# Attention with a block-quantised feed-forward on one core: the work ahead of the first unit in another order, zeros multiplied in TensorE's waits, 22 chunks ahead instead of 24

## The chip, the cores and the metric

One Trainium2 chip, one core of it. The metric is the device time of the program in microseconds (us), the median of a few executions. The change is judged by that time against the kernel before.

## The reference, cut to what is computed

```python
def reference(inputs, Wq, bq, Wk, bk, Wv, bv, Wo, bo, w_gate, w_up, w_down):
    x = inputs                                    # (4, 1024, 128), float32
    xn = layernorm(x)
    # 16 heads of 8; rel[i, j] = pos[j] - pos[i] of one axis, so the bias is a row per head
    q, k, v = split_heads(xn @ Wq + bq), split_heads(xn @ Wk + bk), split_heads(xn @ Wv + bv)
    scores = einsum('bhqd,bhkd->bhqk', q, k) / sqrt(8) + alibi_slopes[:, None, None] * rel
    attn = einsum('bhqk,bhkd->bhqd', softmax(scores), v) @ Wo + bo
    # fp4_linear rounds both operands to a grid of 8 magnitudes, one scale for each 16 elements
    h = silu(fp4_linear(xn, w_gate)) * fp4_linear(xn, w_up)     # 352 wide
    return x + attn + fp4_linear(h, w_down)
```

## The kernel before

The core's four batches are worked off as 256 **units** (`NU`): batch, group of four heads (`quad`), half of the queries, and one of eight blocks of 128 keys. In unit U the stream on TensorE (`pe`) has two **chunks** (`half_chunk`, L1048: queries by all 1024 keys, for the row maxima alone), four **scores** (`score`, L1067) and the **value product** of unit U-1 (`value_product`, L1078). VectorE (`dve`) reduces each chunk to its row maxima (`reduce_chunk`, L934); a chunk has one of two PSUM slots `mx`, and TensorE may write a slot only when the reduction of what stood in it is done. ScalarE (`act`) takes the exponentials (L728). GpSimd (`pool`) does the quantising of the feed-forward and splits the maxima in two bf16 parts (`max_parts`, L630 and L631), which TensorE turns (`turn`, L1056) and SyncE's DMA queue (`sp`) brings into the operands `q_op` by way of DRAM.

The chunks run ahead of the scores: `LEAD` = 24 chunks are done before unit 0 starts.

All other work is a **job**, put into the middle or the end of a unit by `plan()`; at most one job stands in each unit's middle. Jobs are the transposes of the weights (`gT`, `uT`, `dT`), the product `bvo`, the projections of the next batches (`xnT`, `q`, `k`, `v`), the feed-forward of 16 pairs of token tiles (`xT`, `gate`, `up`, `hT`, `down`, beginning with unit `FFN_FIRST`), and the last projection (`ctxT`, `wo`). Each engine goes through its program strictly in order, and the order of one engine is not that of another: a wait on TensorE for a job holds all units behind it. GpSimd walks the same units, with the jobs' follow-up work: `swish`, `hidden`, `scale_to_grid`, `add_power`, `take_power`, `scale_back`, `normalize` of the next batches (in unit 1 for batch 1), `three_parts` (units 16 and 18, 31 and 33, and so on, for q and k of a group).

Before unit 0 stands the **head**: x is loaded, normalised and transposed for the two groups of 512 tokens of batch 0, q and k are projected, each is split into three bf16 parts (`two_parts` on VectorE, `last_parts` on GpSimd), the parts go to DRAM (`parts_to_dram`), and come back as operands (`gather`, one call of four DMAs for each quad). Then come the 24 chunks. In them VectorE also does `powers(0)` (L925), ahead of chunk 8; GpSimd waits for it, and then runs `add_power(0)`, `take_power(0)`, `scale_back(0)`, the clearing of `v_op[1]` (L639, L640), and the loop over units, whose unit 1 has `normalize(2)` and `normalize(3)` (L581). TensorE's job `xnT` of group 2 stands in unit 4 and waits for `xn_ok` to count three groups, which is the end of `normalize(2)`:

```python
    for U, job in enumerate(("bvo", "gT", "uT", "dT")):
        put(U, job)
...
        for g in (2 * b, 2 * b + 1):
            U = norm_unit(b) + 1 + 8 * (g % 2)
            for name in ("xnT", "q", "k"):
                U = put(U + 1, name, g)
```

`put` takes the first free unit from the one that it is given. With the jobs of the weights in units 0 to 3, `xnT` of group 2, which asks for unit 3, gets unit 4.

Of the kernel before, what the change touches and what calls it, by code (L numbers as in the profile page):

```python
# [5 lines left out]
F32 = mybir.dt.float32  # L6
# [64 lines left out]

LEAD = 24
CHUNKS = 2 * B * QUADS * UNITS
HALVES = 2 * B * QUADS
FFN_FIRST, FFN_LAST = 5, 237
# [35 lines left out]
def plan():  # L111
# [11 lines left out]
    for U, job in enumerate(("bvo", "gT", "uT", "dT")):  # L123
        put(U, job)
# [43 lines left out]

def rings():
# [9 lines left out]
    for g in range(2):  # L179
        for name in ("xnT", "q", "k", "v"):  # L180
            to_act(name, g)
    for pos in range(LEAD):
        to_dve("max", pos)
        if pos == 17:
            to_act("turn", 0)
    def to_ring(job):
        (to_dve if job[0] in IN_DVE_RING else to_act)(*job)
# [18 lines left out]
def attn_ffn(nc, x, wq, bq, wk, bk, wv, bv, wo, bo, wg, wu, wd, out):  # L206
    with ExitStack() as ctx:
# [12 lines left out]

        ident = sb("ident", [P, P], F32)
# [61 lines left out]
        x_in = [sem(f"x_in{i}") for i in range(X_LOADS)]  # L283
        ident_ok = sem("ident_ok")
# [6 lines left out]
        dve_step = sem("dve_step")  # L291
        bias_ok = sem("bias_ok")
# [6 lines left out]
        xn_ok = sem("xn_ok")  # L299
        two_parts_ok = sem("two_parts_ok")  # L300
# [58 lines left out]

        @block.sync  # L360
        def _(sp):
            for i in range(2):
                sp.sem_inc(stored[i], 16)
            q_flat = q_rows.rearrange("r c s -> (r c) s")
            k_flat = k_rows.rearrange("r c s -> (r c) s")
# [6 lines left out]
            for g in range(2):  # L372
                x_load(g)
            for dst, src in ((wq_s, wq), (wk_s, wk), (wv_s, wv)):
                sp.dma_start(dst[:], src).then_inc(qkv_in, 16)
            for dst, src in ((bq_s, bq), (bk_s, bk), (bv_s, bv)):
                sp.dma_start(dst[:], src.rearrange("(p a) -> p a", a=1)).then_inc(qkv_in, 16)
            for g in range(2, NG):
                x_load(g)
# [8 lines left out]
            def part_rows(part):  # L388
                return slice(*((0, 3), (3, 5), (5, 6))[part])

            def q_part(g, part):
                to = q_rows[:, part_rows(part), g * GW:(g + 1) * GW]
                sp.dma_start(to, qk_p[g % 2][0][:, part:part + 1, :].to_broadcast([P, to.shape[1], GW])).then_inc(
                    parts_out[g % 2], 16)

            def k_parts(g, part):

                to = k_rows[:, part_rows(part), g * GW:(g + 1) * GW]
                sp.dma_start(to, qk_p[g % 2][1][:, 0:to.shape[1], :]).then_inc(parts_out[g % 2], 16)

            def parts_to_dram(g):
                sp.wait_ge(two_parts_ok, g + 1)
                q_part(g, 0)
                q_part(g, 1)
                k_parts(g, 1)
                k_parts(g, 2)
                sp.wait_ge(parts_ok, g + 1)
                q_part(g, 2)
                k_parts(g, 0)

            def gather(b, quad):
                r0, col = 32 * quad * C, b * S
# [4 lines left out]
                for to, rows in ((q_op, q_flat), (k_op, k_flat)):  # L417
                    for x in range(2):
                        sp.dma_start(to[quad][XROWS * x:XROWS * x + HROWS, :, :],
                                     rows[r0:r0 + 4 * HROWS, col:col + S].rearrange(  # L420
                                         "(g x r) s -> x r g s", g=2, x=2)[x]).then_inc(gathered[quad], 16)
# [54 lines left out]
        def _(pool):  # L476
# [17 lines left out]
            for h in range(H):  # L494
# [3 lines left out]
                           allow_small_or_imprecise_dtypes=True).then_inc(dist_ok, 1)  # L498
            for w in (W_GATE, W_UP):
                nc.gpsimd.memset(w_all[96:P, w + 2 * P:w + 3 * P], 0.0).then_inc(pad_ok, 1)  # L500
            pool.wait_ge(pad_ok, 2)
            for i in range(QUADS):
                nc.gpsimd.memset(k_op[i][:].bitcast(F32), TWO_ONES)
                ins = nc.gpsimd.memset(q_op[i][:].bitcast(F32), TWO_ONES)
            ins.then_inc(ones_ok, 1)

            def last_parts(g):

                i = g % 2
                pool.wait_ge(two_parts_ok, g + 1)  # L510
                nc.gpsimd.tensor_tensor(qk_p[i][0][:, 2, :], qk_r[i][0], qk_p[i][0][:, 1, :], ALU.subtract)
                nc.gpsimd.tensor_tensor(qk_p[i][1][:, 2, :], qk_r[i][1], qk_p[i][1][:, 1, :],
                                        ALU.subtract).then_inc(parts_ok, 1)

            for g in range(2):
                last_parts(g)
# [58 lines left out]
            def normalize(g):  # L575

                b, i = g // 2, g % 2
                pool.wait_ge(ln_ok, 2)
                for t in range(GT):
                    c = (i * GT + t) * P  # L580
                    ins = nc.gpsimd.tensor_scalar(xn_s[b % 2][:, c:c + P], x_s[:, b * S + c:b * S + c + P],  # L581
                                                  rstd[:, g * GT + t:g * GT + t + 1], nmr[:, g * GT + t:g * GT + t + 1],
# [637 lines left out]
```

## Time and profile before

| | |
|---|---|
| median of 3 runs | 858.97 us (858.61 to 860.21) |
| the profiled execution | 858.46 us, of which its span 856.7 us |
| mean granted clock of TensorE | 0.961 |
| busy: PE, DVE, ACT, POOL | 778.5, 695.4, 652.2, 416.5 us |

```profile
## 2 busy tenths in 40 slices
PE   3289998989999999899899999999999999998986
DVE  7797886888989897788888887888888898989710
POOL 7365263482628373662545462761717362442442
PEclk9657998999999999989999999999999999999999
```

A slice is 21.4 us. A digit is the busy share in tenths, and in the row PEclk the granted clock in tenths of full speed (5 is 1.2 GHz, 10 and 9 are at or near 2.4 GHz). The times in the profile count from the first instruction; the profiled execution takes 1.8 us more than its span.

### The profile page before, as it was taken

The numbers are of one execution on the slowest core, as the hardware profiler recorded it, in microseconds if no ns is written. First come the engines' busy times: TensorE is split into PE (matmuls) and PEld (weight loads), VectorE is DVE, ScalarE is ACT, GpSimd is POOL, SyncE is SP. The second block draws the span as 40 slices with busy tenths as digits, with TensorE's granted clock in tenths as the row PEclk, the third lists the DMA queues.
The fourth block names the chain that finished last, engine by engine and source line by source line (L and its number), as shares of the span: only waits on it lengthen the run. The fifth ranks groups of instructions, "written<-read, shape, count | busy, mean of one in ns | idle before, by whom it ended". The sixth has DMA issues, their size and how long they took to land.

```text
span 856.7 us, 13894 instructions
## 1 busy us (share of the span) xinstructions
PE 778.5 (91%) x4939; PEld 232.0 (27%) x4939; DVE 695.4 (81%) x792; ACT 652.2 (76%) x1342; POOL 416.5 (49%) x413
## 2 busy tenths in 40 slices
PE   3289998989999999899899999999999999998986
PEld 2012232223232333222232333222222323232322
DVE  7797886888989897788888887888888898989710
ACT  4206886878888888778788888887888888888885
POOL 7365263482628373662545462761717362442442
PEclk9657998999999999989999999999999999999999
DMA  5920002013102010050101011050102000000000
GB/s 149 243 51 1 2 2 76 2 50 100 39 1 51 2 67 10 14 149 1 39 2 38 3 45 45 2 160 2 38 2 50 3 14 2 2 1 2 2 2 25
DMA packets 32828, 31.85 MB, mean 37 GB/s; under 512 B 4344, under 2 KB 26552, under 8 KB 32760
## 3 DMA queue, kind: packets, MB, share of 16 engines
q1 hardware_dynamic: 32760, 30.96, 13.4%
q8 instruction: 40, 0.66, 0.3%
q14 instruction: 28, 0.23, 0.1%
HBM read 15.91 MB, written 15.04 MB: 36 GB/s over the span
## 4 chain that ended last, share of the span: by engine, by line
PE 66%; DVE 17%; ACT 6%; POOL 6%; issue 3%; DMA 1%; SPq 0%; POOLq 0%; ACTq 0%; DVEq 0%
PE low L1078 23%; PE mx L1048 21%; DVE neg_max L934 13%; PE low L1067 6%; ACT probs L728 4%; PE low L1116 3%; PE low L1101 2%; PE low L1095 2%; PE low L1034 2%; PE mx L1127 2%; PE low L1108 2%; ACT pv_s L825 1%; POOL mb L537 1%; DVE am L905 1%; PE low L1030 1%
## 5 line engine op out<-in xcount | busy, mean ns | idle before, releaser
L934 DVE TENSOR_REDUCE neg_max<-mx 128x1 f32<-128x1024 f32 x512 | 614.1, 1220 | 99.5 <-PE mx L1048 91.4
L728 ACT ACTIVATE probs<-low 128x512 f32<-128x512 f32 x1024 | 558.7, 607 | 141.1 <-PE low L1067 135.2
L1048 PE MATMUL mx<-k_op,q_op 51*128 51x512 bf16 x1024 | 320.1, 398 | 42.0 <-DVE neg_max L934 21.8
L1067 PE MATMUL low<-q_op,k_op 53*128 53x512 bf16 x1024 | 334.4, 389 | 12.7 <-ACT probs L728 9.1
L1078 PE MATMUL low<-probs,v_op 128*32 128x512 f32 x2048 | 275.7, 611 | 0.3
L1048 PEld LDWEIGHTS mx<-k_op,q_op 51*128 51x128 bf16 x1024 | 61.8, 95 | 318.2 <-issue 171.5
L1067 PEld LDWEIGHTS low<-q_op,k_op 53*128 53x128 bf16 x1024 | 74.7, 93 | 91.6 <-ACT probs L728 81.9
L630 POOL CAST neg_parts<-neg_max 128x16 bf16<-128x16 f32 x31 | 6.8, 219 | 167.1 <-DVE neg_max L934 102.1
L537 POOL TENSOR_SCALAR mb<-mb 128x960 f32<-128x960 f32 (+2 forms) x17 | 58.7, 3456 | 27.5 <-DVE mb L925 26.2
L1078 PEld LDWEIGHTS low<-probs,v_op 128*32 128x32 f32 x2048 | 40.5, 108 | 67.5 <-issue 32.2
L618 POOL TENSOR_TENSOR x_s<-x_s,down_s 128x128 f32<-128x128 f32 x32 | 14.6, 455 | 80.5 <-ACT down_s L761 57.9
L611 POOL TENSOR_TENSOR hid<-gate_s,up_s 128x352 f32<-128x352 f32 x32 | 29.9, 935 | 39.6 <-ACT up_s L755 37.4
L526 POOL TENSOR_TENSOR zb<-hid,inv 128x704 f32<-128x704 f32 x16 | 22.2, 1385 | 49.2 <-DVE inv L920 48.5
L605 POOL TENSOR_SCALAR tanh_s<-tanh_s 128x704 f32<-128x704 f32 x16 | 31.7, 1979 | 24.5 <-ACT gate_s L749 22.8
L543 POOL TENSOR_TENSOR zb<-zb,mb 128x960 f32<-128x960 f32 (+2 forms) x17 | 38.2, 2249 | 1.2 <-POOL neg_parts L631 0.4
L538 POOL TENSOR_TENSOR zb<-zb,mb 128x960 f32<-128x960 f32 (+2 forms) x17 | 38.1, 2241 | 1.4
L949 DVE RECIPROCAL pv_r<-mx 128x16 f32<-128x16 f32 x32 | 8.2, 256 | 35.3 <-PE mx L1127 34.9
L734 ACT COPY max_t<-low 32x128 bf16<-32x128 bf16 x32 | 8.2, 255 | 32.9 <-PE low L1056 32.2
L1116 PE MATMUL low<-dT_s,hqT 128*128 128x128 f32 (+1 forms) x192 | 29.6, 291 | 0.0
L606 POOL TENSOR_TENSOR gate_s<-tanh_s,gate_s 128x704 f32<-128x704 f32 x16 | 26.9, 1679 | 1.3
L1095 PE MATMUL low<-gT_s,xqT 128*128 128x352 f32 x64 | 27.5, 511 | 0.0
L1101 PE MATMUL low<-uT_s,xqT 128*128 128x352 f32 x64 | 27.5, 511 | 0.0
(128 smaller groups left out, 589.8 us busy)
## 6 DMA issues: line engine op xcount, KB each, us to landing
q_op<-q_rows SPq DMA_DIRECT2D x32, 192.0 KB, 3.8
k_op<-k_rows SPq DMA_DIRECT2D x32, 192.0 KB, 4.8
q_rows<-qp SPq DMA_DIRECT2D x8, 384.0 KB, 2.6
k_rows<-kp SPq DMA_DIRECT2D x8, 384.0 KB, 2.9
x_s<-in_L_attn_inputs_dram SPq DMA_DIRECT2D x8, 256.0 KB, 3.8
q_rows<-qp SPq DMA_DIRECT2D x8, 256.0 KB, 2.9
k_rows<-kp SPq DMA_DIRECT2D x8, 256.0 KB, 3.1
out_dram<-o_s SPq DMA_DIRECT2D x8, 256.0 KB, 2.6
```

Source lines behind the costliest of these rows:

```text
L537: link(nc.gpsimd.tensor_scalar(m, m, 1.0, ROUND, ALU.max, ALU.mult))
L538: link(nc.gpsimd.tensor_tensor(z, z, m, ALU.add))
L543: link(nc.gpsimd.tensor_tensor(z, z, m, ALU.subtract))
L605: link(nc.gpsimd.tensor_scalar(tanh_s[:], tanh_s[:], 1.0, None, ALU.add))
L728: nc.scalar.activation(probs[U % 3][:, 2 * g + x, :], bank("exp", U, j), ACT.Exp).then_inc(st_free, 1)
L934: nc.vector.tensor_reduce(to, slot("max", pos)[:], AX.X, ALU.max, negate=True).then_inc(mx_free, 1)
L1048: ins = nc.tensor.matmul(slot("max", pos)[:, 512 * kh:512 * kh + 512], q, k, start=True, stop=True)
L1067: nc.tensor.matmul(bank("exp", U, j), k_op[quad][r, g, kt * P:(kt + 1) * P], q_op[quad][r, g, half * HALF:(half + 1) * HALF], start=True, ...
L1078: ins = nc.tensor.matmul(pv[32 * hh:32 * hh + 32, :], v_op[b % 2][:, kt, 4 * quad + hh, :], probs[U % 3][:, hh, :], start=(kt == 0), stop= ...
L1095: nc.tensor.matmul(bank("gate", p, t)[:, 0:I], xqT[:, t * P:(t + 1) * P], gT_s[:], start=True, stop=True).then_inc(st_full, 1)
L1101: nc.tensor.matmul(bank("up", p, t)[:, 0:I], xqT[:, t * P:(t + 1) * P], uT_s[:], start=True, stop=True).then_inc(st_full, 1)
L1116: ins = nc.tensor.matmul(bank("down", p, t)[:, 0:P], hqT[t][0:n, c * P:(c + 1) * P], dT_s[0:n, c * P:(c + 1) * P], start=(c == 0), stop=(c ...
```

## The change

- `plan()`: 22 chunks (`FIRST`) are done before unit 0; chunks 22 and 23 become jobs `late` in units 0 and 1. `bvo` moves to unit 2, `gT`, `uT`, `dT` to units 4 to 6, the feed-forward begins with unit 8 instead of 5 and still has its last pair at 237. `xnT` of group 2 asks for unit 3 as before, and unit 3 is now free.
- Head, order: the projections run xnT 0, xnT 1, q 0, k 0, q 1, k 1, v 0, v 1. The second group of batch 0 is normalised on GpSimd. The first two steps of the bias rows (`alibi`) move from VectorE to ScalarE. The split into parts is signalled for each tensor, no longer for each group.
- Head, DMA: the second load of x, the three k parts of group 1 and the two gathers of q for quad 0 are issued by ScalarE, the rest by SyncE; the clearing and the bias rows of quads 1 to 3 come later.
- VectorE: the statistics of batches 1 to 3 come after the first quantiser step; `norm_scale(1)` stands behind chunk 15 and `powers(0)` behind chunk 16, both among the chunks.
- TensorE: `keep_busy(n)`, n products of a block of zeros, 512 columns each, while it waits in the head, and two after each of the 22 chunks.
- GpSimd: `add_bias` in the fifth unit of a batch instead of the third.

```diff
 LEAD = 24
+FIRST = 22
-FFN_FIRST, FFN_LAST = 5, 237
+FFN_FIRST, FFN_LAST = 8, 237
...
-    for U, job in enumerate(("bvo", "gT", "uT", "dT")):
-        put(U, job)
+    for pos in range(FIRST, LEAD):
+        put(pos - FIRST, "late", pos)
+    put(LEAD - FIRST, "bvo")
+    for i, name in enumerate(("gT", "uT", "dT")):
+        put(4 + i, name)
...
+PROJECTIONS = [("xnT", 0), ("xnT", 1), ("q", 0), ("k", 0), ("q", 1), ("k", 1), ("v", 0), ("v", 1)]
...
             sp.wait_ge(bias_ok, 1)
             sp.dma_start(bias_rows, bias_p).then_inc(bias_out, 16)
+            sp.wait_ge(bias_out, 16)
             sp.wait_ge(ones_ok, 1)
-            sp.wait_ge(bias_out, 16)
-            for quad in range(QUADS):
-                bias_rows_in(quad)
+            bias_rows_in(0)
             for g in range(2):
                 parts_to_dram(g)
-            for quad in range(QUADS):
+            gather(0, 0)
+            for quad in range(1, QUADS):
+                sp.wait_ge(ones_ok, quad + 1)
+                bias_rows_in(quad)
                 gather(0, quad)
...
+            clear_operands(0)
             for w in (W_GATE, W_UP):
                 nc.gpsimd.memset(w_all[96:P, w + 2 * P:w + 3 * P], 0.0).then_inc(pad_ok, 1)
             pool.wait_ge(pad_ok, 2)
...
+            normalize(1)
+            clear_operands(1)
             for g in range(2):
-                last_parts(g)
+                for j in range(2):
+                    last_part(g, j)
+            for i in range(2, QUADS):
+                clear_operands(i)
...
-                if u == 2 and b < B:
+                if u == 4 and b < B:
                     add_bias(b)
...
+            act.dma_start(x_s[:, GW:2 * GW].rearrange("p (t e) -> p t e", e=E),
+                          x_tok[GT:2 * GT].rearrange("t p e -> p t e")).then_inc(x_in[0], 16)
             std(0)
+            alibi()
             act.wait_ge(qkv_in, QKV_IN)
...
+            normalize()
+            for name, g in PROJECTIONS:
+                {"xnT": keep_xnT, "q": keep_q, "k": keep_k, "v": keep_v}[name](g)
+                if (name, g) == ("k", 1):
+                    act.wait_ge(two_parts_ok, 4)
+                    k_rows_out(act, 1, 1)
+                    k_rows_out(act, 1, 2)
+                    act.wait_ge(parts_ok, 4)
+                    k_rows_out(act, 1, 0)
+            act.wait_ge(ones_ok, 1)
+            for i in range(2):
+                act.wait_ge(parts_out[i], PARTS_IN)
+            for x in range(2):
+                gather_rows(act, q_op, q_rows, 0, 0, x)
             std(1)
...
+            nc.vector.memset(warm[:], 0.0).then_inc(warm_ok, 1)
             mark(nc.vector.memset(v_op[0][:], 0.0))
+            load_stats(0)
             norm_stats(0)
...
-            norm_stats(1)
-            norm_scale(1)
             weight_maxima()
             x_maxima(0)
             block_scales(0)
             block_inverses(0)
-            for pos in range(LEAD):
-                if pos == 8:
+            for load in range(2, X_LOADS):
+                load_stats(load)
+            norm_stats(1)
+            for pos in range(FIRST):
+                reduce_chunk(pos)
+                if pos == 15:
+                    norm_scale(1)
+                if pos == 16:
                     powers(0)
-                reduce_chunk(pos)
...
+            def keep_busy(n):
+                for _ in range(n):
+                    nc.tensor.matmul(pv, warm[:, 0:P], warm[:], start=True, stop=True)
+
+            pe.wait_ge(warm_ok, 1)
+            pe.wait_ge(x_in[0], 16 * NG // X_LOADS)
+            keep_busy(8)
             pe.wait_ge(ident_ok, 1)
-            project("xnT", 0)
-            pe.wait_ge(qkv_in, QKV_IN)
...
+            pe.wait_ge(ln_ok, 1)
+            keep_busy(4)
+            for name, g in PROJECTIONS:
+                if (name, g) == ("q", 0):
+                    pe.wait_ge(qkv_in, QKV_IN)
+                project(name, g)
+            pe.wait_ge(two_parts_ok, 4)
+            keep_busy(6)
+            pe.wait_ge(parts_ok, 4)
+            keep_busy(6)
+            for i in range(2):
+                pe.wait_ge(parts_out[i], PARTS_IN)
+            keep_busy(12)
+            for pos in range(FIRST):
                 for kh in range(2):
                     half_chunk(pos, kh)
+                keep_busy(2)
                 if pos == 17:
                     turn(0)
```

## Rows read from the trace of the kernel before

**Rows 1.** The chain that ended last, cut to 0 to 130: start, us, what.

```profile
10.09 1.66 ACT xn_s L688 x4
...
28.31 3.34 DMA k_rows<-kp
...
33.03 4.82 DMA k_op<-k_rows
...
39.05 9.39 DVE neg_max L934 x8
...
73.33 1.86 PE low L1078 x8
...
77.54 0.99 PE low L1078 x8
...
83.43 0.99 PE low L1078 x8
```

**Rows 2.** Windows: stretch, its length, busy (x count) by engine, PEclk, DMA share, GB/s.

```profile
28.00:30.00 2.00, 0.00 (x0) 0.00 (x0) 1.97 (x12) 0.00 (x0) 0.55 (x2) 0.50 0.98 342
...
38.00:48.00 10.00, 7.85 (x18) 1.02 (x18) 8.97 (x8) 0.00 (x0) 2.12 (x3) 0.50 1.06 200
...
135.00:140.00 5.00, 4.45 (x20) 1.09 (x20) 2.45 (x2) 2.91 (x6) 0.27 (x2) 0.51 0.12 39
140.00:145.00 5.00, 5.00 (x34) 1.70 (x31) 3.19 (x3) 3.35 (x7) 0.00 (x0) 0.81 0.80 280
```

**Rows 3.** Timeline of the head: start, us, engine, line, what [idle before <- releaser].

```profile
1.64 3.47 DVE L961 MEMSET v_op<- 128x4096 f32 x1 [1.64 <-PEq L1208]
...
13.73 2.05 PE L1034 MATMUL low<-xnT_s,wq_s 128*128 128x512 f32 x2 [0.77 <-ACT xnT_s L698]
...
20.41 0.92 SPq L393 DMA_DIRECT2D q_rows<-qp  x2
20.42 1.10 PE L1034 MATMUL low<-xnT_s,wq_s 128*128 128x512 f32 x2 [0.82 <-ACT xnT_s L698]
...
22.71 0.69 ACT L712 ACTIVATE kp<-low,bk_s 128x512 bf16<-128x512 f32 x1
...
24.74 0.43 DVE L887 CAST kp<-gate_s 128x512 bf16<-128x512 f32 x1
...
32.11 0.30 DVE L867 RECIPROCAL ln<-ln 128x24 f32<-128x24 f32 x1 [0.36 <-ACT ln L681]
...
33.53 0.18 DVE L873 TENSOR_SCALAR nmr<-ln 128x24 f32<-128x24 f32 x1
...
48.35 1.00 DVE L925 TENSOR_SCALAR mb<-zb 128x1632 int32<-128x1632 int32 x1
...
49.44 5.69 POOL L537 TENSOR_SCALAR mb<-mb 128x1632 f32<-128x1632 f32 x1 [9.32 <-DVE mb L925]
```

**Rows 4.** Timeline, 56 to 110: GpSimd's chain ends, TensorE in the first units.

```profile
69.68 0.60 PE L1048 MATMUL mx<-k_op,q_op 51*128 51x512 bf16 x1 [0.42 <-DVE neg_max L934]
...
69.86 3.46 POOL L581 TENSOR_SCALAR xn_s<-x_s,rstd,nmr 128x128 f32<-128x128 f32 x8
...
70.08 0.63 PE L1048 MATMUL mx<-k_op,q_op 51*128 51x512 bf16 x1
...
81.95 0.66 PE L1024 MATMUL low<-ident,xn_s 128*128 128x128 f32 x4
...
84.39 0.09 PEld L1048 LDWEIGHTS mx<-k_op,q_op 51*128 51x128 bf16 x1 [0.48 <-issue]
```

**Rows 5.** Timelines of GpSimd and TensorE, 126 to 140, round a stall.

```profile
133.39 1.15 POOL L596 TENSOR_TENSOR kp<-kr,kp 128x512 bf16<-128x512 f32 x1
...
135.55 0.27 PE L1056 MATMUL low<-ident_b,neg_parts 128*32 128x128 bf16 x1 [2.40 <-POOLq L633]
```

**Rows 6.** Timelines of VectorE and TensorE, 350 to 375, round another stall.

```profile
360.82 0.52 DVE L905 TENSOR_REDUCE am<-hid 128x22 f32<-128x352 f32 x1 [2.21 <-POOLq L612]
...
362.53 0.39 PE L1048 MATMUL mx<-k_op,q_op 51*128 51x512 bf16 x1 [2.85 <-DVE neg_max L934]
```

More of the change, by code:

```diff
@@ L177, in to_dve @@
         dve[key] = len(dve)
-    for g in range(2):
-        for name in ("xnT", "q", "k", "v"):
-            to_act(name, g)
-    for pos in range(LEAD):
+    for name, g in PROJECTIONS:
+        to_act(name, g)
+    for pos in range(FIRST):
         to_dve("max", pos)
@@ L186, in to_ring @@
     def to_ring(job):
+        if job[0] == "late":
+            to_dve("max", job[1])
+            return
         (to_dve if job[0] in IN_DVE_RING else to_act)(*job)
@@ L370, in x_load @@
                                  x_in[g * X_LOADS // NG], 16)
[L372 to L374 removed]
+            x_load(0)
+            for dst, src in ((wq_s, wq), (wk_s, wk)):
                 sp.dma_start(dst[:], src).then_inc(qkv_in, 16)
@@ L416, in gather @@
                     sp.wait_ge(parts_out[i], (b + 1) * PARTS_IN)
[L417 to L421, printed above, removed]
+                for x in range(2):
+                    gather_rows(sp, k_op, k_rows, b, quad, x)
+                    if b or quad:
+                        gather_rows(sp, q_op, q_rows, b, quad, x)
             def bias_rows_in(quad):
@@ L498, in _, with clear_operands, last_part, normalize @@
                            allow_small_or_imprecise_dtypes=True).then_inc(dist_ok, 1)
+            def clear_operands(i):
+                mark(nc.gpsimd.memset(k_op[i][:].bitcast(F32), TWO_ONES))
+                mark(nc.gpsimd.memset(q_op[i][:].bitcast(F32), TWO_ONES))
+                settle()
+                pool.sem_inc(ones_ok, 1)
+            def last_part(g, j):
+                pool.wait_ge(two_parts_ok, 2 * g + j + 1)
+                nc.gpsimd.tensor_tensor(qk_p[g][j][:, 2, :], qk_r[g][j], qk_p[g][j][:, 1, :], ALU.subtract).then_inc(parts_ok, 1)
+            def normalize(g):
+                b, i = g // 2, g % 2
+                pool.wait_ge(ln_ok, min(b, 1) + 1)
+                for t in range(GT):
+                    c = (i * GT + t) * P
+                    mark(nc.gpsimd.tensor_scalar(xn_s[b % 2][:, c:c + P], x_s[:, b * S + c:b * S + c + P],
+                                                 rstd[:, g * GT + t:g * GT + t + 1], nmr[:, g * GT + t:g * GT + t + 1],
+                                                 ALU.mult, ALU.add))
+                settle()
+                if g == 1:
+                    pool.sem_inc(xn1_ok, 1)
+                    pool.wait_ge(xn_ok, 1)
+                pool.sem_inc(xn_ok, 1)
+            clear_operands(0)
             for w in (W_GATE, W_UP):
@@ L573, in add_bias @@
                 ins.then_inc(xb_ok, 1)
[L575 to L582, printed above, removed]
-                                                  ALU.mult, ALU.add)
-                ins.then_inc(xn_ok, 1)
             def three_parts(g, j, name):
@@ L1144, in job_on_array @@
                     ins.then_inc(st_full, 1)
+                elif kind == "late":
+                    for kh in range(2):
+                        half_chunk(p, kh)
                 elif kind == "bvo":
```

130 lines of the change are left out of this document (63 added, 67 removed).

## The prediction

> **What bounds the kernel now.** I read four views in this order: the windows for the clock and the DMA share, the chain that ended last cut to the first 130 us, the timeline of the head engine by engine, and the timelines round the later stalls.
>
> The chain's first part is a latency path: normalising on ScalarE from 10.09, the projections, the copies and the splitting, then the parts' way to DRAM (the last issue at 28.31 has landed at 31.65), then the gather (issued up to 33.03, landed at 37.85) [rows 1]. From 39.05 on VectorE reduces chunks back to back: 8 take 9.4 us, so 1.175 us each, and TensorE waits for slots [rows 1, 3]. The granted clock is 0.50 in all of that [rows 2], which costs nothing in the head, as the two products of a chunk start 0.40 us apart [rows 4], but does in the first units: a value product takes 1.86 us at 73.33 and 0.99 at 77.54, and the distance from one to the next is 4.21 us at the lower level and 2.95 (two units in 5.89) at the higher one [rows 1]. From there on the units take about 2.95 us, held by the coupling of TensorE and ScalarE, and two long stalls stand in them: TensorE is idle 2.40 us at 135.5 for `max_parts`, which GpSimd reaches only after `three_parts` of k [rows 5], and 2.85 us at 362.5, since VectorE waited 2.21 us for `hidden`, late by `three_parts` of q [rows 6].
>
> What the reader should see beside the chain: GpSimd's own chain. It starts when `powers(0)` is done (49.35), L537 starts at 49.44 [rows 3], and `normalize(2)` starts at 69.86 [rows 4], 20.42 us later; its four instructions are half of the 3.46 us, so TensorE's job `xnT` of group 2 could go at 71.6. It goes at 81.95 [rows 4]. That slack of 10 us is why the chain isn't on the path now.
>
> **The change part by part.** All of the head is first put as the start of the first reduction, called R: 39.05 before.
>
> Start: VectorE clears the 512 columns of `warm` ahead of `v_op`. 4096 float columns take 3.47 us [rows 3], so 512 take at most 0.43, and the statistics, which start as that ends, come 0.45 later. ScalarE gets two passes over 1024 columns of the bias rows between `std(0)` and the normalising. No row shows one; 512 columns take 0.69 [rows 3], so a pass is between 0.69 and 1.38, and I take 1.1, as the fixed part isn't doubled. They begin at about 8.5 and end at 10.8; the scaling of bq follows, and normalising starts near 11.15 instead of 10.09: 1.05 us late. That move frees nothing that anybody waits for.
>
> Projections: two transposes then run ahead of q 0, and ScalarE becomes the bound: four tensors q 0, k 0, q 1, k 1 by two copies of 0.69, 5.5 us. A pair of f32 products of 512 columns takes 2.05 us on the cold array and 1.10 later [rows 3]. If the eight zeros have brought the clock up, k 1 is kept at 20.8 and split at 21.95; if it comes up only during q, 2.3 us later. Before, the split ended at 25.17 [rows 3]. The v copies, 0.6 each, are no longer ahead of it. I take 23.1.
>
> Parts to DRAM: 3 MB. Issues began at 20.41 [rows 3], and with the DMA engines at a share of 0.98 and 342 GB/s [rows 2] the last landed at 31.65, 11.2 us after the first issue. Now the first issue follows the first tensor's split, 5.3 us ahead of the last split less one, at 17.8 to 19.7. The stream needs 3.07 MB / 340 GB/s = 9.0 us and about 1.6 of start and landing: 28.9 to 30.8, taken as 29.5, a gain of 2.1. The engines have no spare share in this stretch, so that ScalarE issues three of the twelve brings no bandwidth. The Trainium skill ("Trainium Kernel Development and Optimization", Key Constraints) says of the queues of the issuing engines that all run on the same 16 DMA engines and that issuing from several saves the sequencer's issue time alone; by that rule this part gives no more than I count. A reader who takes two queues for twice the rate would put this stream at half, some 4.5 us earlier.
>
> Gather of quad 0: before, 31.65 to 37.85, 6.2 us. Four issues of 0.43 become two on each of two queues (0.8 less), quads 1 to 3 follow as before, and 768 KB at 200 GB/s [rows 2] stay 3.8 us. I take 5.5, bounds 5.2 and 6.2. TensorE starts chunk 0 at 35.0; the reduction starts 0.6 to 1.05 later. R = 35.7, with 34.4 and 37.2 as ends: 3.3 us gained. The twelve zeros in the gather take 12 x 0.4 = 4.8 us at the lower level [rows 4], which the gather hides; without that cover they would cost what stands over it.
>
> Chunks: two zeros after each make four products, at the lower level 4 x 0.40 = 1.6 us for 1.175 of reduction, at the higher one half of that. As TensorE is then without a gap at the lower level, I expect the clock up after a chunk or two (0.5 us) and count nothing for the rest. `norm_scale(1)` was hidden ahead of chunk 0 (seven instructions, 32.11 to 33.71 [rows 3]); it now stands among the chunks, where VectorE is the bound: 1.6 us on the path. Two chunks leave the head, 2.35 us, and come back in units 0 and 1, where three reductions (3.5 us) are longer than a unit's 2.95.
>
> The moved `powers(0)` is the step that I put the sum on. Before it started after 8 chunks; L537 stood at R + 10.4. Now it starts after 17 reductions (20.0), the parts of the maxima (0.34), `norm_scale(1)` (1.65) and itself (1.05): R + 23.1. Behind it GpSimd's queue is unchanged: `add_power`, `take_power`, `scale_back`, clearing `v_op[1]`, `normalize(2)`: 20.42 + 1.73 + 0.1 = 22.25. So xnT 2 can't run before R + 45.35 = 81.1. And it now stands in unit 3, not 4. TensorE would be there at about R + 38.5: unit 0 can start when the 21st reduction is done, R + 27.8, and the reductions of units 0 to 2 go on without a gap to there. So TensorE stands still for 7 us ahead of xnT 2, with all units behind it, whatever the head has gained; the DMA gain counts only in R.
>
> From xnT 2 on, against before: then it ran at 81.95 and unit 5 began at 84.39 [rows 4], 2.44 later. Now the rest of unit 3 (2.44 at the higher level) and unit 4 (2.95) come first, and after a stand of 7 us they run at the lower level. A unit costs 4.21 there against 2.95 [rows 1]; after the stall at 135 the clock was low from 135.5 to 141.9, as 0.81 in 140 to 145 is 1.9 us at 0.50 [rows 2]; for such 6.5 us that is 6.5 x (1 - 2.95/4.21) = 1.95. Unit 5 begins at 81.1 + 0.1 + 2.44 + 2.95 + 1.95 = 88.55: 4.15 later than before. At its start before, all three weight jobs were done; now `uT` and `dT` are still to come, and lengthen two units by some 0.17 each: 0.35.
>
> Later: with the feed-forward 3 units later, `grid` and `pow` of pair 0 meet `three_parts` of q and k in units 16 and 18 closer to `max_parts` of unit 19: GpSimd reaches it 3.1 us late instead of 2.4, +0.7. Pair 5's `hidden` is queued behind `three_parts` of q by one unit less, and VectorE waits 1.0 instead of 2.2: the idle 2.85 becomes some 1.6 and the clock stays up; -2.5. `add_bias` in unit 68 now meets pair 3's `add_power`, so hT of pair 3 in unit 72 waits: +0.7. The end has hT and down one unit later, where no chunks or scores run: -0.2 (one down product comes to lie under VectorE's step).
>
> **The sum**: 4.15 + 0.35 + 0.7 - 2.5 + 0.7 - 0.2 = 3.2 us. The profiled execution of 858.46 would be 861.7; on the median of 858.97, 0.5 above it, 862.2.
>
> **The rivals.**
>
> A: the gain of the head comes through, and nothing stands in unit 3. That takes GpSimd's chain to end by R + 38.5: it would have to be 7 us shorter than the 22.25 that its rows add up to, or TensorE be held elsewhere. For it: the units 0 to 3 run at the higher clock. Time: unit 4 starts at R + 41 = 76.7 against 81.4, -4.7, and with 0.35 and the -1.3 of the later parts -5.7: 853.3. Between this and the forecast the point is the end of `normalize(2)` against TensorE's middle of unit 3. Chance 0.12.
>
> B: the zeros don't raise the clock, or not for good, and then they are a load: 1.6 to 1.7 us a chunk for 1.175, over 17 chunks 7.5 to 9 us on R + 23.1, and all behind it. Time 870. Against it: at the lower level there's no gap. Chance 0.08. A milder form has the clock go down and up within the chunks, half the chunks at either level: 866, chance 0.08. The Trainium skill ("TensorE: Matmul & The Clock Gate", the section on psum-queue depth-cycling) describes that: short idle times between groups of matmuls at the turn of PSUM banks make the clock oscillate. By that rule the 866 would be likelier; the trace of before shows a steady 0.50 in this stretch [rows 2], and no row here shows zeros.
>
> C: the shifted feed-forward. If the stall at 135 goes too, or the one at 362 stays with its dip, the sum moves by -3 or +2.5: 859 or 865. Chance 0.12 for the first, within the forecast's width for the second.
>
> **How the numbers follow.** Forecast 0.60, at 862.2; its own width is from R (-1.3 to +1.5) and the later stalls (-1.5 to +2.5): 859.5 to 866. A 0.12, B 0.16, C's low case 0.12. Left out of the range are half of A's low end and the full form of B: 856 to 868.5. 0.2% is 1.7 us, about what a measurement of this kernel can tell from no change. Faster by more: A and a quarter of C, 0.15. Within: the rest of C and the forecast's lowest end, 0.13. Slower: 0.72.
>
> **What would show it.** In the profile after: the first reduction near 35.7; L925 near 57.8 and L537 near 58.9; the transposes of L1024's second use (xnT 2) near 81 with an idle time of about 7 us ahead of them, released by GpSimd; PEclk at 0.50 for some 6 us behind it; the idle of 2.4 before the fourth `turn` grown to 3, and that at 362 shrunk. Wrong would make it: `normalize(2)` ending before TensorE is in unit 3, or chunks 1.6 us apart in the whole head.

## The result, and the profile after

The changed kernel takes 874.43 us (median of 4 runs, 873.17 to 876.06) beside 859.08 for the kernel before on the same chip (4 runs, 858.61 to 860.21): ratio 1.0185, 95% interval 1.0157 to 1.0213. That is slower, as forecast, but by 15.4 us and not by 3.2: outside the range. Its profiled execution took 873.20 us with a span of 871.1, against 858.46 and 856.7 before.

First the windows of the changed kernel, to be read beside those of the kernel before [rows 2] (columns as there).

```profile
33.00:37.00 4.00, 0.02 (x1) 0.00 (x0) 0.55 (x7) 1.71 (x3) 1.13 (x2) 1.00 1.06 188
38.00:48.00 10.00, 10.00 (x22) 1.30 (x20) 6.67 (x6) 0.00 (x0) 0.00 (x0) 0.50 0.96 191
48.00:58.00 10.00, 10.00 (x22) 1.43 (x22) 6.46 (x6) 0.00 (x0) 0.00 (x0) 0.50 0.01 2
58.00:68.00 10.00, 10.00 (x22) 1.30 (x20) 6.39 (x8) 0.00 (x0) 0.00 (x0) 0.50 0.00 0
68.00:78.00 10.00, 10.00 (x22) 1.41 (x21) 8.20 (x14) 0.25 (x1) 6.12 (x2) 0.50 0.01 2
78.00:88.00 10.00, 9.15 (x33) 1.49 (x34) 8.28 (x7) 4.34 (x8) 9.84 (x5) 0.50 0.00 0
...
93.00:98.00 5.00, 3.85 (x27) 1.40 (x27) 2.96 (x4) 3.18 (x7) 3.78 (x10) 1.00 0.02 5
```

In 38 to 48 TensorE was busy 7.85 us before and is busy 10.00 now, with VectorE at 6.67 instead of 8.97: the bound has moved from VectorE to TensorE, and the granted clock is 0.50 (1.2 GHz) in every window from 38 to 88, although TensorE shows no idle time at all up to 78. The chain that ended last says the same (start, us, what):

```profile
26.00 4.13 DMA k_rows<-kp
...
30.61 6.33 DMA q_op<-q_rows
...
38.44 0.96 PE mx L1102 x2
39.40 0.97 PE low L1226 x2
...
65.50 0.98 PE mx L1102 x2
...
71.79 5.70 POOL mb L583
...
...
94.11 0.63 PE low L1078 x4
```

Before, eight `neg_max` stood there in one piece of 9.39 us [rows 1]. Now the chain runs over TensorE alone: a chunk's two products (0.96) and its two zeros (0.97) make 1.93 us, to the sixteenth chunk. Then comes `add_power` (L583) at 71.79, the instruction that was L537 at 49.44 [rows 3], and the transposes of `xnT` 2 at 94.11, 81.95 before [rows 4].

The timeline of the changed kernel has the steps of the head and the three places further on ([rows 3, 5, 6] for before):

```profile
10.64 4.11 POOL L543 TENSOR_SCALAR xn_s<-x_s,rstd,nmr 128x128 f32<-128x128 f32 x4 [0.67 <-DVE nmr L919]
...
18.94 1.63 POOL L535 TENSOR_TENSOR qp<-qr,qp 128x512 bf16<-128x512 f32 x1 [2.10 <-DVE qp L930]
19.58 1.27 DVE L930 CAST kp<-kr 128x512 bf16<-128x512 f32 x1
...
37.09 0.59 PE L1102 MATMUL mx<-k_op,q_op 51*128 51x512 bf16 x2 [4.07 <-DMA q_op<-q_rows]
37.71 1.23 DVE L976 TENSOR_REDUCE neg_max<-mx 128x1 f32<-128x1024 f32 x1 [4.13 <-PE mx L1102]
...
94.11 0.63 PE L1078 MATMUL low<-ident,xn_s 128*128 128x128 f32 x4 [1.78 <-POOLq L550]
...
99.04 0.22 PE L1110 MATMUL low<-ident_b,neg_parts 128*32 128x128 bf16 x1
...
152.97 0.27 PE L1110 MATMUL low<-ident_b,neg_parts 128*32 128x128 bf16 x1 [4.38 <-POOLq L667]
...
308.69 0.52 PE L1162 MATMUL low<-ident,hq 128*128 128x128 f32 x3 [2.10 <-POOLq L611]
...
377.10 0.52 DVE L947 TENSOR_REDUCE am<-hid 128x22 f32<-128x352 f32 x1 [1.93 <-POOLq L646]
...
378.81 0.39 PE L1102 MATMUL mx<-k_op,q_op 51*128 51x512 bf16 x1 [1.30 <-DVE neg_max L976]
```

The turn of unit 4 makes a good milestone, as from there both kernels do nearly the same: 99.04 here, 84.24 before, 14.8 us later. The last turn stands at 828.59 against 815.33 (13.3 later), and the spans differ by 14.4. So all of the loss arises before 99 us, and what follows gives back 0.4 on balance: 1.5 up to the last turn, less 1.1 behind it.

### The profile page after: what moved, and what is told of

It is laid out like the page before. It is cut to its first block, busy times and chain, and to the rows that moved or that the text cites. A ratio compares the mean times of both kernels' runs of the same rounds, so it can differ in the third digit from the quotient of the medians.

```text
span 871.1 us, 14078 instructions
## 1 busy us (share of the span) xinstructions
PE 807.4 (93%) x5019; PEld 236.9 (27%) x5019; DVE 695.8 (80%) x791; ACT 652.2 (75%) x1340; POOL 420.7 (48%) x417
## 4 chain that ended last, share of the span: by engine, by line
PE 67%; DVE 15%; POOL 8%; ACT 5%; issue 3%; DMA 1%; ACTq 0%; POOLq 0%; DVEq 0%
PE low L1132 23%; PE mx L1102 22%; DVE neg_max L976 10%; PE low L1121 6%; ACT probs L766 3%; PE low L1170 3%; PE low L1155 3%; PE low L1149 2%; PE mx L1181 2%; PE low L1226 2%; POOL mb L583 1%; PE low L1162 1%; ACT pv_s L870 1%; PE low L1088 1%; DVE am L947 1%
## 5 line engine op out<-in xcount | busy, mean ns | idle before, releaser
L583 POOL TENSOR_SCALAR mb<-mb 128x960 f32<-128x960 f32 (+2 forms) x17 | 58.8, 3456 | 58.4 <-DVE mb L967 57.5
L1226 PE MATMUL low<-warm 128*128 128x512 bf16 x80 | 35.0, 567 | 11.9 <-DMA x_s<-in_L_attn_inputs_dram 5.2
L772 ACT COPY max_t<-low 32x128 bf16<-32x128 bf16 x32 | 8.1, 254 | 45.2 <-PE low L1110 44.5
```

The costliest lines, as they stand in the source:

```text
L583: link(nc.gpsimd.tensor_scalar(m, m, 1.0, ROUND, ALU.max, ALU.mult))
L1226: nc.tensor.matmul(pv, warm[:, 0:P], warm[:], start=True, stop=True)
```

## The experiments

The theory was: two zeros behind each chunk, on an array that has just fallen to 1.2 GHz in the gather's wait, make TensorE the bound of the chunk loop, and the loop delays `powers(0)` and with it everything. Without them, the forecast's own stall ahead of `xnT` 2 is left. All ratios are to the kernel before, run beside each kernel on the same chip.

**Without the zeros between chunks.**

```
             for pos in range(FIRST):
                 for kh in range(2):
                     half_chunk(pos, kh)
-                keep_busy(2)
```

> The changed kernel without the two products of zeros after each chunk; the zeros in the waits stay. Theory (zeros are a load at 1.2 GHz): chunks come 1.18 us apart again instead of 1.93, the first unit starts about 16 us earlier, but xnT of group 2 can still run only 45.4 us after the first reduction, so TensorE then stands idle about 7 us ahead of it and the clock falls once more: 861 to 864 us. Rival (the zeros cost nothing, the reductions were slow for another reason): 874 us, chunks still 1.9 us apart. Second rival (GpSimd's chain isn't what TensorE waits for): no long idle time ahead of xnT, 853 to 856 us.

Measured: 866.64 us, ratio 1.0091 [1.0074, 1.0108]. From its timeline:

```profile
39.28 1.04 PE L1102 MATMUL mx<-k_op,q_op 51*128 51x512 bf16 x4 [4.62 <-DMA q_op<-q_rows]
...
63.19 5.69 POOL L583 TENSOR_SCALAR mb<-mb 128x1632 f32<-128x1632 f32 x1 [27.46 <-DVE mb L967]
...
85.56 1.09 PE L1078 MATMUL low<-ident,xn_s 128*128 128x128 f32 x4 [4.54 <-POOLq L550]
```

The first reduction starts at 40.34; L583 follows 22.85 us behind it (forecast 23.1; the changed kernel has 34.1) and `xnT` 2 45.2 behind it (forecast 45.35), with TensorE idle for 4.54 us. This kernel is the one that I had forecast, 4.6 us later in its first reduction: 862.2 + 4.6 = 866.8 against 866.6. That it agrees so closely is partly luck, as the idle time is 4.54 us and not 7, and what comes behind unit 4 gives back less than I had forecast; but the steps are right. The zeros in the loop cost 7.8 us.

**The zeros alone, in the kernel before.**

```
             for pos in range(LEAD):
                 for kh in range(2):
                     half_chunk(pos, kh)
+                keep_busy(2)
```

> The kernel before, with only the two products of zeros after each of its 24 chunks added. If they are the load, a chunk takes 1.93 us instead of 1.18 as the clock is at 1.2 GHz when the chunks start and, by the changed kernel's trace, doesn't come back in them: 22 gaps more of 0.75 us, 16 to 18 us above the kernel before, 875 to 877 us. If what kept the clock down in the changed kernel is something else in its head, the clock rises within some 7 us and the sum is 860 to 863 us.

Measured: 874.54 us, ratio 1.0192 [1.0163, 1.0222]. Two of its windows:

```profile
38.00:48.00 10.00, 10.00 (x22) 1.30 (x20) 6.12 (x5) 0.00 (x0) 2.01 (x3) 0.50 0.91 190
48.00:58.00 10.00, 10.00 (x22) 1.44 (x22) 7.00 (x7) 0.00 (x0) 3.62 (x1) 0.50 0.00 0
```

Chunks are 1.93 us apart here too and the level stays 0.50. 24 chunks by 1.93 - 1.175 are 18 us; 15.9 arrive at the end. Nothing else of the change is in this kernel, so the loss belongs to the zeros and the loop.

**Is it what is multiplied?**

```
-            nc.vector.memset(warm[:], 0.0).then_inc(warm_ok, 1)
+            nc.vector.memset(warm[:], 1.0).then_inc(warm_ok, 1)
```

> The changed kernel with ones in place of zeros in the products. If the clock depends on the data (zeros don't count as work), it is back at 2.4 GHz within some 7 us of the first chunk and the time falls by 8 us or more, to 866 or less. If it depends only on what the array does and when, nothing changes: 873 to 876 us.

Measured: 875.03 us (2 runs), ratio 1.0192 [1.0172, 1.0212]. Ones do as zeros do.

**The wait for the gather filled.** The array is at 1.00 in 33 to 37, idle for 4.07 us there, and at 0.50 behind that. With 32 zeros in place of 12 it isn't idle:

```
             for i in range(2):
                 pe.wait_ge(parts_out[i], PARTS_IN)
-            keep_busy(12)
+            keep_busy(32)
```

> The changed kernel with 32 products of zeros in place of 12 in the wait for the gather, so that TensorE isn't idle in the 4.1 us ahead of the first chunk. Theory A (the clock falls after the idle 4.1 us, and stays down since products of 51 rows and of zeros in turn don't bring it back, but would hold it): granted clock 1.0 through all 22 chunks, 1.18 us apart, and then as e1 with an idle time ahead of xnT of about 7 us: 860 to 863 us. Theory B (the mixed stretch neither raises nor holds it): the clock falls a few us into the chunks, 872 to 875 us.

Measured: 864.87 us, ratio 1.0073 [1.0058, 1.0088]. Its windows:

```profile
40.00:50.00 10.00, 9.85 (x37) 2.07 (x38) 10.00 (x10) 0.00 (x0) 0.00 (x0) 1.00 0.96 186
50.00:60.00 10.00, 8.90 (x32) 1.77 (x31) 9.72 (x17) 0.26 (x1) 0.00 (x0) 1.00 0.01 3
60.00:65.00 5.00, 3.63 (x9) 0.61 (x10) 5.00 (x5) 0.00 (x0) 3.23 (x1) 0.65 0.02 3
```

The same instructions now run at 2.4 GHz for over 20 us (1.00 in 40 to 60), VectorE is the bound again (10.00 of 10), and the level falls only after TensorE has waited for `norm_scale(1)` and `powers(0)`. So the loop's mix kept the level that it found here, and didn't bring it back where it had gone. The zeros in the loop cost nothing in this profile: `add_power` starts 22.3 us behind the first reduction, 22.9 without them. What is left of the loss stands at the late `powers(0)`: TensorE waits 2.30 us ahead of `xnT` 2 at 84.12.

**`powers(0)` back behind eight chunks**, still without zeros in the loop, `norm_scale(1)` where the change has it:

```
             for pos in range(FIRST):
+                if pos == 8:
+                    powers(0)
...
-                if pos == 16:
-                    powers(0)
```

> As the run before, and the step powers(0) ahead of chunk 8 as in the kernel before, so that GpSimd's chain starts about 11 us earlier. Theory: the idle time of 7 us ahead of xnT of group 2 is gone, 8 to 10 us less than the run before, 852 to 855 us. Rival (the chain isn't the cause): the same time as the run before within 1 us.

Measured: 867.23 us, ratio 1.0101 [1.0085, 1.0117]: no gain, against my expectation. The idle time ahead of `xnT` 2 is gone and another one has come. From the timeline, VectorE, GpSimd and TensorE:

```profile
59.67 3.65 POOL L589 TENSOR_TENSOR zb<-zb,mb 128x1632 f32<-128x1632 f32 x1
...
60.08 3.28 DVE L914 TENSOR_TENSOR ln<-ln 128x24 f32<-128x24 f32 x1
...
63.40 2.14 POOL L594 TENSOR_TENSOR w_all<-zb,sc 128x1120 f32<-128x1120 f32 x1
63.61 1.96 DVE L916 TENSOR_SCALAR ln<-ln 128x24 f32<-128x24 f32 x1
...
68.13 2.17 PE L1102 MATMUL mx<-k_op,q_op 51*128 51x512 bf16 x4 [7.41 <-DVE neg_max L976]
```

L914 and L916, 24 columns each, take 3.28 and 1.96 us; the same L914 takes 0.18 at 68.40 in the changed kernel. Each ends within 0.05 us of GpSimd's instruction beside it (63.32 and 63.36, 65.54 and 65.57). The two are not slowed, one waits for the other to end. The Trainium skill has this ("SBUF — State Buffer", the section on who interferes with whom): VectorE and GpSimd share a pair of ports under an exclusive lock, taken by VectorE's instructions with two SBUF inputs or in a two-port mode, and the later one is blocked until the earlier ends. The trace agrees to 0.05 us. With `norm_scale(1)` among the chunks, its seven small steps stand in front of the reductions: they take 7.2 us (59.75 to 66.95), where they take 1.6 in the changed kernel with GpSimd idle, and TensorE waits 7.4 us.

**Both ahead**: `norm_scale(1)` in front of the first chunk, in the gather's shadow, where before had it, and `powers(0)` behind eight.

```
+            norm_scale(1)
             for pos in range(FIRST):
+                if pos == 8:
+                    powers(0)
...
-                if pos == 15:
-                    norm_scale(1)
-                if pos == 16:
-                    powers(0)
```

> As e1, with norm_scale(1) ahead of the chunks and powers(0) ahead of chunk 8. In e2, where norm_scale(1) stood behind chunk 15, VectorE's instructions of L914 and L916 took 3.3 and 2.0 us while GpSimd ran add_power. Theory (these were held by GpSimd's instruction, and the chain's idle time was only replaced by that): with norm_scale(1) out of the way both are gone, 857.5 to 860.5 us, clock 0.50 in the chunks. Rival (L914 waits for something else, such as the square root of ScalarE): it takes as long ahead of the chunks, and the first chunk's reduction is 3 us or more later than in e2.

Measured: 859.05 us, ratio 1.0007 [0.9988, 1.0026]. L583 starts at 50.38, the turn of unit 4 at 85.64, and L914 takes 0.18 us at 35.88, so it waited for GpSimd and not for ScalarE's square root. Moving seven small instructions is worth 8.2 us: some 5.6 of it is what the lock added to them in the run before, most of the rest their own 1.6 (an estimate from the two lengths above).

With this run the loss of 15.4 us can be divided: 7.8 go with the zeros in the loop, 7.6 with the places of `norm_scale(1)` and `powers(0)`, and the rest of the change together is worth nothing that can be told from zero (859.05, ratio 1.0007).

**The stall taken from the other end**: TensorE's order changed so that `xnT` 2 is asked for later, without zeros in the loop and with `powers(0)` late as in the change.

```
     for i, name in enumerate(("gT", "uT", "dT")):
-        put(4 + i, name)
+        put(3 + i, name)
```

> As e1 (no zeros between the chunks), with gT, uT and dT in units 3, 4 and 5, by which xnT of group 2 stands in unit 6 instead of 3. Theory (e1 lost 5.5 us of idle time ahead of xnT and a fall of the clock behind it): neither is there, 859 to 862 us against 866.6 of e1. Rival (what follows would wait as well, for GpSimd's quantised weights ahead of gT): 864 to 867 us.

Measured: 861.43 us, ratio 1.0044 [1.0029, 1.0059], 5.2 us below the kernel with the same VectorE order and `xnT` in unit 3. Its transposes, now behind a turn that stands at 87.97 instead of 92.62, have no idle time ahead:

```profile
91.91 0.66 PE L1078 MATMUL low<-ident,xn_s 128*128 128x128 f32 x4
```

**Clock and order together**: the filled wait, zeros in the loop, both pieces of VectorE's work ahead.

```
+            norm_scale(1)
             for pos in range(FIRST):
+                if pos == 8:
+                    powers(0)
...
-            keep_busy(12)
+            keep_busy(32)
```

> The changed kernel with 32 products of zeros in the wait for the gather, norm_scale(1) ahead of the chunks and powers(0) ahead of chunk 8. Theory: the granted clock is 1.0 all through the chunks and units, neither GpSimd's chain nor VectorE's small steps hold anybody, unit 4 starts some 2.5 to 3 us earlier than in the kernel before: 854.5 to 857 us. Rival (the clock falls once the wait is over): above 862 us.

Measured: 859.77 us, ratio 1.0034 [1.0001, 1.0067]. The level is 1.00 to 69.5 us and then gone:

```profile
65.00:70.00 5.00, 2.98 (x16) 0.67 (x16) 5.00 (x6) 3.21 (x6) 4.79 (x5) 0.95 0.00 0
70.00:75.00 5.00, 4.90 (x20) 0.88 (x18) 3.40 (x4) 1.86 (x5) 3.66 (x9) 0.50 0.01 3
```

Units 0 and 1 have no zeros and carry three chunks instead of two, so VectorE's reductions bound them and TensorE waits some 0.5 us for each. The ten runs lie in two groups, seven at 857.4 to 861.0 (mean granted clock 0.979 to 0.987) and three at 866.7 to 868.1 (0.966 to 0.969); the profile is of the first. So keeping the clock through the loop alone is worth nothing (median of the seven 859.3, against 859.05 without the zeros), and in three of ten executions this kernel is 8 us slower, which the one without zeros in the loop never was in its ten (857.95 to 862.09).

**The later quads' gathers held back.** The head's gain had not come either, so SyncE waits for quad 0's rows before it issues the others' gathers:

```
             gather(0, 0)
+            sp.wait_ge(gathered[0], GATHERED)
             for quad in range(1, QUADS):
```

> The kernel with no zeros in the chunk loop and the POOL work moved ahead (859.05 us before this run), and besides SyncE waits for quad 0's rows to be in before it issues the gathers of quads 1 to 3. In that kernel the first chunk starts 6.3 us after the first gather was issued although quad 0's own four gathers are alone 0.77 MB at some 340 GB/s, and SyncE issues six more gathers of the later quads from 33.4 us on. Theory: these share the DMA engines with quad 0's q rows, which wait in ScalarE's queue; with them held back the rows are in 5.2 us after the first issue, the first reduction starts 1 us earlier and the time falls by 0.7 to 1.2 us. Rival: the gather's length is its own (many short packets); it stays 6.2 to 6.5 us and the time moves by under 0.3 us. In either case quads 1 to 3 are not late: unit 16's scores want quad 1 only at 130 us.

Measured: 858.80 us, ratio 1.0003 [0.9990, 1.0017], beside 859.05 without the wait. From its chain:

```profile
32.22 6.38 DMA q_op<-q_rows
...
38.73 0.65 PE mx L1102 x4
```

6.93 us from the first issue (31.80) to the first product, 7.17 without the wait. My theory that the later gathers are in the way is wrong by this: holding them gave 0.24 us of the 1 that I expected. What sets the gather's length isn't shown; in the kernel before it was 6.27 from the first issue (31.71) to the first product.

**The feed-forward's grid.** The two stalls further on, 4.4 us ahead of a turn and 2.1 ahead of an `hT`, looked like two tasks of GpSimd that meet in a unit. By the units of the planner, tasks don't meet there on a grid from unit 11:

```
-FFN_FIRST, FFN_LAST = 8, 237
+FFN_FIRST, FFN_LAST = 11, 237
```

> The kernel with no zeros in the chunk loop and the POOL work moved ahead (859.05 us), and besides the FFN's first job in unit 11 in place of 8 (the last still in 237). Theory: the two stalls that the FFN's new grid brought, TensorE waiting 4.4 us for POOL's max_parts at the turn near 139 us and 2.1 us for an hT near 295 us, are collisions of two POOL tasks in one unit; on the grid from unit 11 the tasks fall apart, both stalls are gone, and the time falls by 4 to 6 us, to 853 to 855. Rival: the units around them are bound by DVE and ScalarE and take the time back, or the collision comes at another unit: 857 to 860, with a stall of over 2 us elsewhere.

Measured: 850.53 us (848.83 to 851.31), ratio 0.9909 [0.9895, 0.9924]: 8.5 us below the same kernel with 8. The same two TensorE instructions in its timeline, with nothing ahead of them:

```profile
132.75 0.22 PE L1109 MATMUL low<-ident_b,neg_parts 128*32 128x128 bf16 x1
...
294.77 0.55 PE L1161 MATMUL low<-ident,hq 128*128 128x128 f32 x3
```

The gain is 2 us more than the two stalls. It isn't the head's: from the turn of unit 4 to the last one this kernel takes 722.1 us against 731.0. Part of the rest is the clock behind a stall, since the kernel with 8 has 0.51 in 140 to 145:

```profile
140.00:145.00 5.00, 5.00 (x24) 1.11 (x20) 2.73 (x3) 2.96 (x7) 3.76 (x3) 0.51 0.31 101
```

**The same number in the kernel before**, to see to whom that gain belongs:

```
-FFN_FIRST, FFN_LAST = 5, 237
+FFN_FIRST, FFN_LAST = 11, 237
```

> The kernel before with one number changed: the FFN's first job in unit 11 in place of 5, the last still in 237. The changed kernel without zeros between chunks, with the POOL work ahead and the FFN from unit 11 takes 850.5 us; this tells how much of that belongs to the FFN's grid alone. Theory: the kernel before has the same kind of collisions (2.4 us ahead of the turn near 135.6 us, 2.85 us ahead of the job near 362.5 us), the same grid takes both away, and it falls by 4 to 6 us to 852.5 to 854.5; the work ahead of the first unit as rearranged is then worth 2 to 4 us. Rival: units 4 to 10 gain nothing from the missing FFN jobs and the grid collides with the work of units 1 to 3 as it lies in this kernel: 857 to 859, with a wait for POOL of over 2 us left; then the rearranged head is worth 7 us or more together with this grid.

Measured: 851.77 us (847.61 to 853.75), ratio 0.9901 [0.9876, 0.9927]. The turn that waited 2.40 us [rows 5] waits for nothing (first line, of the timeline), and where a product waited 2.85 us for a reduction [rows 6], the longest such wait of TensorE is now 1.3 (second line, of the waits: total, times, longest):

```profile
134.61 0.22 PE L1056 MATMUL low<-ident_b,neg_parts 128*32 128x128 bf16 x1
```

```profile
PE mx L1048 <- DVE neg_max L934: 18.1, 36, 1.3
```

The two intervals lie on each other. So the grid is worth 8 us in either kernel, and the reordered head, repaired, nothing that these runs can tell from zero. That the stalls are gone is shown; that they were tasks of GpSimd meeting in one unit is read from the planner and from what released the waits, and only the one other grid was tried.

**All together**: filled wait, zeros in the loop, in unit 0 and in the first half of unit 1, VectorE's work ahead, gathers held, feed-forward from unit 11.

```
+                    if 2 * U + i < 3:
+                        keep_busy(2)
                     if 0 < U <= NU and i == 1:
                         value_product(U - 1)
```

> The kernel with the gather wait filled (32 zeros), zeros between chunks and the POOL work ahead (859.8 us), and besides: two zeros behind the scores in units 0 and the first half of 1, the later quads' gathers held until quad 0's are in, and the FFN from unit 11. Theory: the clock, which fell at 69.5 us in units 0 and 1 where TensorE waits 0.5 us for DVE at each chunk, stays at 1.0, and the turn of unit 4, 84.8 us there and 84.2 us in the kernel before, comes at 80 to 82 us; with the two later stalls gone too the time is 848 to 854, below both kernels. Rival: the zeros push the scores of units 0 and 1 back and the units behind are bound by DVE's reductions, which no clock makes shorter: the turn of unit 4 stays at 84 to 85 us and the time at 854 to 857.

Measured: median 856.24 us, ratio 0.9933 [0.9900, 0.9967], but 12 runs lie in two groups, five at 846.6 to 848.0 and seven at 855.8 to 858.4. The profiled execution is of the first (847.76), and there the level holds through units 0 and 1:

```profile
65.00:70.00 5.00, 4.50 (x23) 0.99 (x22) 5.00 (x6) 3.26 (x6) 4.79 (x5) 1.00 0.00 0
70.00:75.00 5.00, 3.64 (x27) 0.95 (x30) 4.50 (x6) 2.55 (x5) 3.61 (x9) 1.00 0.01 3
```

The turn of unit 4 comes at 81.50, and from there to the last turn it takes 722.1 us like the kernel with only the grid. So zeros can be worth some 3 us where they keep a level that is there and fill time that is idle, and cost some 6 in the other seven executions. No profile fell in the second group, but its mean granted clock is on record: 0.976 to 0.980, against 0.992 to 0.997 in the first. A difference of 0.016 over 855 us is some 28 us more at 1.2 GHz (an estimate: 0.016 x 855 / 0.5). A level lost while the filler runs on, as in the changed kernel, would fit; where it is lost isn't shown. The steadier kernel, 850.5 with its five runs in a spread of 2.5, is the better one to keep.

## Why the prediction failed, step by step

**The chunk loop's zeros** are the step that failed. I wrote that TensorE, without a gap at the lower level, would have its clock back after a chunk or two, "and count nothing for the rest". It had no gap from 38 to 78 us (busy 10.00 of 10 in each window), and stayed at 1.2 GHz from about 38 to 89. L583 came 34.1 us behind the first reduction, forecast 23.1: 11 us. I had drawn "no gap at the lower level" as the argument against rival B; it was exactly what B's load looks like. B's mechanism was right, at 0.08, and its price too small: I took 0.40 us a product from two that start 0.40 apart [rows 4], where four back to back take 0.48 each, 1.93 us a chunk and not 1.6 to 1.7. Its 870 becomes 874 to 875 with that: 17 chunks by the 0.23 to 0.33 that was missing are 4 to 5.6 us. That this meets the measured 874.4 is partly luck, as the 2.0 us of the late first reduction and the 2.4 that came back behind `xnT` 2 (both below) nearly cancel. The Trainium skill ("TensorE: Matmul & The Clock Gate", on what is actually happening) lets the level follow how busy the array has been of late; the windows show an array busy without a gap at the lower level for 40 us, so the rule as put there doesn't cover this mix. Its oscillation by idle times between PSUM banks, which I had weighed as the milder rival, isn't seen either: the level is steady.

**The start of the first reduction** was forecast at 35.7 (34.4 to 37.2) and is 37.71. The parts landed at 30.15 (forecast 29.5), inside my bounds. The gather took 6.7 us from its first issue (30.20) to its landing (36.94) and 6.9 to the first product, where I had 5.5 and at most 6.2; before, on one queue, it took 6.2 to its landing. So splitting it over two queues brought nothing. Two things that I hadn't counted stand on the path to the last split, which ends at 24.64 and not at 23.1: GpSimd's four normalising instructions take 4.11 us (four take 1.74 at 92.18), and VectorE's casts 1.27 beside GpSimd's `last_part`, 0.43 alone [rows 3]. Each of these casts ends 0.3 us behind the GpSimd instruction beside it, so waits for the shared ports are the likely cause; no run tested it here.

The rest depends on the execution. I had the eight zeros ahead of the projections bring the array up; here they did (first line), in the kernel with both pieces of work ahead they didn't (the other two):

```profile
15.34 1.02 PE L1088 MATMUL low<-xnT_s,wq_s 128*128 128x512 f32 x2
```

```profile
15.79 1.91 PE L1087 MATMUL low<-xnT_s,wq_s 128*128 128x512 f32 x2
...
39.97 1.22 DVE L976 TENSOR_REDUCE neg_max<-mx 128x1 f32<-128x1024 f32 x1 [2.83 <-PE mx L1101]
```

Of the eleven kernels profiled with this head, two have q 0's pair at 1.02 us and the first reduction at 37.7 to 37.8; nine have it at 1.91 to 1.92 and the first reduction at 39.4 to 40.3, no earlier than the 39.05 before. So in most executions the 3.3 us that I had the head gain aren't there at all.

**GpSimd's chain** held to the digit: L583 to `xnT` 2 was forecast 22.25 and is 22.3, in the kernel without zeros 22.4. In that one the forecast stall is there too, 4.54 us; 7 was too much, as TensorE reached it 40.7 us behind the first reduction and not 38.5. In the changed kernel it is only 1.78, since the zeros held TensorE up as well.

**Behind `xnT` 2** I had 7.45 us to unit 5, with 1.95 for a low clock; the clock was 1.00 there (93 to 98), the turn ahead of unit 5 comes 4.93 behind it, and that gives 2.4 back. In the kernel without zeros in the loop, with its longer stand of 4.54 us, the term holds: 7.06 to the same turn, with a granted clock of 0.50 in 85 to 91. To the turn of unit 4: 2.0 by the first reduction, 11.0 by the loop, -2.4 here, 10.6 of the 10.65 that it misses.

**The later parts** came out at -0.4 from that turn on, forecast -0.95: at the job that was at 362 (now 377.10) VectorE waits 1.93 us where I had 1.0, TensorE 1.30 in place of 2.85, and from the turn ahead of it to the one behind it 2.7 us are given back where I had 2.5; the stall ahead of the fourth turn grew to 4.38 and not to 3.1, and `hT` of pair 3 waits 2.10 where I had 0.7. I priced these collisions one by one as small change around a fixed grid. The grid itself was the largest lever in sight, 8 us.

**Rival A** had 853.3 for a head whose gain comes through. No kernel with the grid of this change reached it; the best was 858.8. The kernel with both pieces of work ahead has no idle time of TensorE ahead of `xnT` 2, as A wanted, but its first reduction is at 39.97 and not at 35.7, and the clock is low to 80: A failed by the head's gain, not by GpSimd's chain.

## What to carry to other kernels

Filler on TensorE is a load as soon as the array is at its lower level: price it at that level, back to back (0.48 us for 512 columns here), against what the other engine needs for the same step, and assume that the level it finds is the one it will have. Fill the whole of a wait or none of it: here a filler that ended 4 us short left the array low and the filler behind it on the path. And look at the spread, not at one profile: two of the three kernels with the filled wait were 8 to 10 us slower in some of their executions.

When work is moved among engines, follow what runs beside it: small VectorE instructions beside long GpSimd ones can wait for those to end (3.28 us in place of 0.18 here), and the place with nothing on GpSimd is the cheap one.

Where a periodic schedule meets an aperiodic one, try the offset first: one number moved the kernel before by 8 us, more than all that was rearranged in the head.

## What the runs showed of the hardware beyond that

- The same stream, two products of 51 rows and two of 128 rows over 512 columns, stayed at 0.50 for some 40 us, to its end, when the level fell at its start (changed kernel, kernel before with zeros, ones for zeros) and at 1.00 for over 20 us when it began there (filled wait). Why a busy array isn't raised wasn't settled.
- In each of the thirteen profiles in which the level was low by the end of the chunks or in units 0 and 1, the clock rose only after the value product of unit 0 had started, 1.3 to 8.3 us behind it: in the changed kernel the product starts at 85.98 and the granted clock is 0.50 in 88 to 89 and 0.97 in 89 to 90; before, it starts at 73.33 and the clock rises at 77.0. Whether these products are what raises it wasn't tested.
- Products of zeros and of ones gave the same time, 874.4 and 875.0.
- A VectorE instruction of 24 columns took 3.28 us in place of 0.18 beside a GpSimd one, and ended with it to 0.05 us.
- 768 KB gathered on two queues took no less time than on one: 6.7 us to the landing against 6.2 before.
- The same head runs in two ways: with the same zeros ahead of it, a pair of f32 products took 1.02 us in two profiles and 1.91 to 1.92 in nine.
